# Attention scores by 32-row matmul tiles in four PSUM banks, and transposed probabilities in the turning banks

## What is computed

```python
def _L0_gnn_ref(x, adj_matrix, edge_attr_matrix, ...):
    nx = _ln(x, ln1_g, ln1_b)
    q = (nx @ wq + bq).reshape(b, s, H, HD).transpose(0, 2, 1, 3)      # H = 8, HD = 32; k and v alike
    bias = jnp.where(adj_matrix > 0, 0.1 * edge_attr_matrix * adjf, -jnp.inf)[:, None]
    scores = jnp.einsum('bhqd,bhkd->bhqk', q, k) / np.sqrt(HD) + bias
    attn = jax.nn.softmax(scores, axis=-1)
    out = jnp.einsum('bhqk,bhkd->bhqd', attn, v).transpose(0, 2, 1, 3).reshape(b, s, d)
    x1 = x + (out @ wo + bo)
    return x1 + jax.nn.gelu(_ln(x1, ln2_g, ln2_b) @ w1 + b1, approximate=False) @ w2 + b2

def _L1_gnn_ref(x, adj, ...):                  # attention again, with its own weights and mask adj == 0
    y = attention(x) @ Wo + bo + x
    return (y - mu) * jax.lax.rsqrt(var + EPS) * gamma + beta
```

## Time and profile before

| | |
|---|---|
| Median of 3 executions | 2414.14 us (2414.06 to 2414.62) |
| Profiled execution, its own time | 2410.11 us |
| Span of its core | 2408.0 us |
| TensorE matmul busy | 2332.9 us (97%) |
| TensorE weight loads busy | 1995.6 us (83%) |
| VectorE busy | 1940.4 us (81%) |
| ScalarE busy | 1694.6 us (70%) |
| GpSimd busy | 1106.0 us (46%) |

### The profile page before, as it was taken

How to read it: one execution, slowest core, us unless ns; L and a number is a source line. 1 busy time by engine, 2 the same in 40 slices (tenths; PEclk the granted TensorE clock), 3 DMA queues, 4 the chain that set the end, 5 groups by cost and what they waited for, 6 DMA issues and landing times.

```text
span 2408.0 us, 54142 instructions
## 1 busy us (share of the span) xinstructions
PE 2332.9 (97%) x17728; PEld 1995.6 (83%) x17728; DVE 1940.4 (81%) x8492; ACT 1694.6 (70%) x5646; POOL 1106.0 (46%) x1160
## 2 busy tenths in 40 slices
PE   4799999999999999999999999999999999999996
PEld 4688888888888888888888888888888888888875
DVE  5588888888888888888888888888888888888775
ACT  2567777777777777777777777777777777777774
POOL 2235444454454454454454454454454454454454
PEclk8899999999999999999999999999999999999999
DMA  4122212222212222212222212232222232222211
GB/s 129 36 68 71 71 47 59 79 78 66 71 47 61 77 79 65 71 49 66 70 80 65 71 50 66 69 80 65 71 54 62 69 80 65 73 57 59 58 49 42
DMA packets 172627, 159.35 MB, mean 66 GB/s; under 512 B 16832, under 2 KB 168000, under 8 KB 172352
## 3 DMA queue, kind: packets, MB, share of 16 engines
q1 hardware_dynamic: 172352, 155.91, 24.3%
HBM read 55.20 MB, written 16.78 MB: 30 GB/s over the span
## 4 chain that ended last, share of the span: by engine, by line
PE 88%; DVE 6%; ACT 2%; issue 1%; POOL 0%; POOLq 0%; DVEq 0%; ACTq 0%
PE p_bank L1029 56%; PE p_scores L1029 14%; PE p_probs L1122 8%; PE p_bank L1136 6%; PE p_bank L1047 4%; DVE x_two L708 3%; ACT scores L592 1%; DVE queries_a L817 1%; DVE scores L793 1%; DVE heads_t L863 1%; ACT heads_t L633 1%; DVE negmax L793 0%; DVE normed L813 0%; DVE x_two L742 0%; PE p_bank L980 0%
## 5 line engine op out<-in xcount | busy, mean ns | idle before, releaser
L542 POOL TENSOR_TENSOR scores<-scores,inverse 128x512 f32<-128x512 f32 x512 | 540.9, 1059 | 732.7 <-DVE inverse L803 732.7
L592 ACT ACTIVATE scores<-scores,negmax 128x128 f32<-128x128 f32 x2048 | 792.6, 391 | 23.1 <-DVE negmax L793 19.3
L592 ACT ACTIVATION_READ_ACCUMULATOR scores<-scores,negmax 128x1 f32 x2048 | 388.4, 190 | 0.0
L1029 PEld LDWEIGHTS p_bank<-w_down,hidden 128*128 128x128 f32 x3072 | 374.7, 191 | 8.9 <-issue 6.0
L1029 PE MATMUL p_bank<-w_down,hidden 128*128 128x256 f32 x3072 | 381.8, 284 | 0.0
L1029 PE MATMUL p_bank<-normed,w_up 128*128 128x512 f32 x1536 | 366.7, 395 | 1.9 <-DVE normed L813 1.9
L1029 PEld LDWEIGHTS p_bank<-normed,w_up 128*128 128x128 f32 x1536 | 285.3, 189 | 61.0 <-issue 2.1
L633 ACT ACTIVATE heads_t<-p_bank 128x256 fp32r<-128x256 f32 x256 | 98.6, 385 | 323.2 <-PE p_bank L1136 323.2
L1122 PE MATMUL p_probs<-ident,scores 128*128 128x128 f32 x2048 | 272.6, 276 | 2.8 <-POOL scores L542 2.8
L1122 PEld LDWEIGHTS p_probs<-ident,scores 128*128 128x128 f32 x2048 | 228.0, 141 | 33.4 <-issue 20.0
L616 ACT ACTIVATE p_bank<-p_bank,ready_cols 128x512 f32<-128x512 f32 x256 | 169.5, 662 | 122.0 <-PE p_bank L1029 116.3
(11 more groups left out here) (112 smaller groups left out, 3968.1 us busy)
## 6 DMA issues: line engine op xcount, KB each, us to landing
key_blocks<-hidden SPq DMA_DIRECT2D x512, 128.0 KB, 2.4
x_in<-in_x SPq DMA_DIRECT2D x32, 512.0 KB, 4.4
res_a<-in_x SPq DMA_DIRECT2D x32, 512.0 KB, 4.0
res_c<-x_two SPq DMA_DIRECT2D x32, 512.0 KB, 3.4
out<-res_c SPq DMA_DIRECT2D x128, 128.0 KB, 1.8
adj_a<-in_adj SPq DMA_DIRECT2D x32, 256.0 KB, 3.8
adj_c<-in_adj SPq DMA_DIRECT2D x32, 256.0 KB, 3.2
res_c<-in_L_gnn_w SPq DMA_DIRECT2D x1, 512.0 KB, 5.9
```

Source lines behind the costliest of these rows:

```text
L542: nc.gpsimd.tensor_tensor(rows_c, rows_c, inverse[:, k % 2, heads].unsqueeze(2).broadcast_to([P, HC, P]), ALU.mult).then_inc(probs_made, 1)
L592: last = nc.scalar.activation(scores[:, k % 2, h], scores[:, k % 2, h], ACT.Exp, scale=-1.0, bias=negmax[:, k % 2, h:h + 1], accum_out=tot ...
L1029: last = nc.tensor.matmul(dst, stationary(i), moving(j), start=(n == 0), stop=(n == total_n - 1))
```

## The change

The scores of each head are now a product of their own that reads 32 partitions of the queries and of the keys: 2 halves (c) x 3 passes x 4 heads (j), 24 matmuls with 128 columns. The head's place j sets the rows of the array and the bank: `p_scores` has four banks, one for each j, so that four neighbouring matmuls use four row groups and four banks. `key_blocks`, its DMAs and the waits for them go, and `keys` get tensors of their own for A and C. VectorE's mask waits once for all eight heads and then goes by groups g of four heads (j = 0, 1 and j = 2, 3), where it went by c.

With four banks for scores, `p_probs` goes. The two halves of a unit's transposes, (T, r, 0) and (T, r, 1), now each take one of the four turning banks. The orders change: TensorE makes T after `early` and `mid`, with W between the two halves. VectorE masks its second half before it evacuates the last step's Q1 or K1, and copies the second T half (`turned`) before it evacuates this step's Q0 or K0. ScalarE evacuates `early` and `mid`, then copies the first T half, then makes the second half of the exponentials (in the step with DOWN 1 it makes them first).

```diff
@@ Shape.__init__: numbering of the turning banks
-            self.number(self.first.get(k, []) + only("V", lag) + self.early.get(k, [])
-                        + self.mid.get(k, []) + only("W", lag) + self.fill.get(k, []))
+            self.number(self.first.get(k, []) + only("V", lag) + self.early.get(k, []) + self.mid.get(k, [])
+                        + [op + (0,) for op in only("T", lag)] + only("W", lag) + [op + (1,) for op in only("T", lag)]
+                        + self.fill.get(k, []))
...
-        p_scores = ctx.enter_context(nc.psum_tensor("p_scores", [P, KC, HC * P], F32))
-        p_probs = ctx.enter_context(nc.psum_tensor("p_probs", [P, KC, HC * P], F32))
+        p_scores = ctx.enter_context(nc.psum_tensor("p_scores", [P, HC, TOK], F32))
...
+        def score_columns(c, j):
+            return p_scores[:, j, c * P:(c + 1) * P]
+        def slot_of(c, j):
+            return HC * (j // 2) + 2 * c + j % 2
...
@@ VectorE body
-                    for op in s.fill.get(k - 1, []):
-                        if op[0] in ("Q", "K"):
-                            evacuate(t, op)
                     if k in s.units and k == s.behind:
                         mask_scores(t, k, 0)
                     if k in s.units:
                         mask_scores(t, k, 1)
+                    for op in s.fill.get(k - 1, []):
+                        if op[0] in ("Q", "K"):
+                            evacuate(t, op)
...
-                    for op in s.early.get(k, []):
+                    for op in s.early.get(k, []) + s.mid.get(k, []):
                         if op[0] == "DOWN":
                             prepare(t, k)
-                        evacuate(t, op)
+                        if op[0] in ("DOWN", "UP"):
+                            evacuate(t, op)
                     for _, r in only("T", lag):
                         turned(t, r)
+                    for op in s.early.get(k, []) + s.mid.get(k, []):
+                        if op[0] not in ("DOWN", "UP"):
+                            evacuate(t, op)
                     if k in s.units and k != s.behind:
                         invert(t, k, 1)
-                    for op in s.mid.get(k, []):
-                        evacuate(t, op)
...
@@ TensorE make_scores
-                    moving = lambda j: key_blocks[:, c, j, :, b * P:(b + 1) * P]
-                    stationary = lambda i: queries[stage][:, i, c, b * P:(b + 1) * P]
-                    three_passes(p_scores[:, c, :].rearrange("p (h n) -> p h n", h=HC), [(stationary, moving)]
-                                 ).then_inc(scores_made, 1)
+                    for n, (i, i2) in enumerate(passes):
+                        for j in range(HC):
+                            rows_j = slice(HD * j, HD * (j + 1))
+                            last = nc.tensor.matmul(score_columns(c, j), queries[stage][rows_j, i, c, tokens],
+                                                    keys[stage][rows_j, i2, c, tokens], start=(n == 0),
+                                                    stop=(n == len(passes) - 1))
+                last.then_inc(scores_made, 1)
+            def turn(t, r, g):
+                pe.wait_ge(probs_made, u * KC + g + 1)
+                bank, dst = take(t, ("T", r, g))
+                for n in range(HC):
+                    last = nc.tensor.transpose(dst[:, n * P:(n + 1) * P], scores[:, par, HC * g + n, :], ident[:, :])
+                last.then_inc(filled[bank], 1)
...
@@ TensorE body
-                    for op in s.early.get(k, []):
+                    for op in s.early.get(k, []) + s.mid.get(k, []):
                         work(t, op)
-                    for op, r in only("T", lag):
-                        lagging(t, op, r)
-                    for op in s.mid.get(k, []):
-                        work(t, op)
+                    for _, r in only("T", lag):
+                        turn(t, r, 0)
                     for op, r in only("W", lag):
                         lagging(t, op, r)
+                    for _, r in only("T", lag):
+                        turn(t, r, 1)
```

More of the change, by code:

```diff
@@ L187, in bank, with turned_bank @@
         return n % BANKS, self.grown(n // BANKS + 1, len(s.use) // BANKS)
+    def turned_bank(self, r, g):
+        key = ("T", r, g)
+        if key in self.s.use:
+            return self.bank(key)
+        return self.bank(("T", r + len(self.s.before.order), g), earlier=True)
     def high(self, key):
```

124 lines of the change are left out of this document (47 added, 77 removed).

## The result

The changed kernel takes 2713.56 us (median of 4 runs, 2706.93 to 2717.33), where the kernel before took 2414.10 us beside it. The ratio is 1.124 (95% interval 1.122 to 1.126): 12.4% slower. My forecast of 2664 us was 50 us too low, inside its range.

A forecast was written before the change was run, and what follows sets the result against it. TensorE was taken as the bound, 71.83 of 71.98 us a turn. Some 12.7 us of new waits less 4.9 of shorter scores made +7.8 us a turn, 250 us over 32 turns: 2664 us, range 2500 to 2880.

The forecast's parts named there:

- A block of scores, 0.86 us: The 24 score matmuls on TensorE: 0.86 us at O's pace of 0.036 us each, against 1.47 before.
- Steps 1 and 6, +1.80 each: W waits for K1's or Q1's evacuation, Q1 for Q0's behind the late T copy: 8.32 us against 6.52.
- Steps 0 and 5, +1.71 and +2.51: K0 waits for XT's low part, then W and K1 for banks: +1.71 us in step 0, +2.51 in step 5.
- Step 3, +0.69: UP 0 starts at 1.18 us; UP 2 waits for UP 1's bank: 1.30 less 0.61 is +0.69 us.
- Step 4, -0.61: Only shorter scores; DOWN 1 covers mask and exponentials, and W, T and XT find banks drained: -0.61 us.
- Steps 2 and 7, -0.05: W is held back until 3.14 us, but ScalarE empties V0 in time: 6.63 against 6.68 us, -0.05 each.
- The DMAs of `key_blocks` without effect: Dropping these DMAs saves nothing: they lay beside a busy TensorE, which had 0.15 us without work a turn.
- Busy 85 to 90%: Sign to look for: TensorE's busy share falls to some 85 to 90%, at a granted clock near 1.00.
- "I put nothing down for it": No cost for a clock drop in TensorE's new gaps, though worst steps idle some 2.4 of 8.3 us.
- the covered waits: Rival: bank waits are covered and busy time decides; 2258 us, or about 2320 if VectorE bounds; 14 in 100 together.
- That tiles don't overlap: Rival: row tiles run one after another, scores take 3.1 us, 3240 us in all; 6 in 100.
- the waits would be half of what I walked: Rival: VectorE gets ahead of the walk, or scores reach their lower bound: 2400 to 2500 us; 8 in 100.

The follow-up runs named there:

- the wide scores: Kernel before, with its six 512-column score matmuls and `key_blocks`, but the changed kernel's banks and orders: 2771.22 us, ratio 1.148.
- the second experiment: Changed kernel with the last step's Q1 or K1 evacuated by VectorE ahead of the second half of the mask: 2613.26 us, ratio 1.083.
- the two-bank version: Kernel before, its banks and orders kept, with row tiles in two score banks, heads one behind the other, without `key_blocks`: 2577.86 us, ratio 1.069.
- full rows: Changed kernel with each of the 24 score matmuls reading all 128 rows instead of 32 (another result): 3106.38 us, ratio 1.287.
- the scores twice: Changed kernel with every block of scores made twice, 48 matmuls into the same banks: 2807.22 us, ratio 1.163.

## Why the prediction was right, and where it was off

The predicted 2664 us is 50 us (1.9%) below the measured 2713.56, and the range held it. By its steps:

- **A block of scores, 0.86 us:** 0.82 measured. The estimate from O was right, and so was its reason, that tiles overlap: a 128-column matmul costs 0.11 us on its rows, and four go at once. My other price, 0.13 us overlapped by four, gave 0.79 and was as near. *The gain of 0.61 us a step* was a little too large, since the entry into row tiles was not counted (0.17 us behind XT).
- **Steps 1 and 6, +1.80 each:** step 1 took 8.44 us against 6.52, +1.92. The chain ahead of Q1 was 2.04 us for 2.07 walked. From the early T to W it was 1.15 us for 0.40 + 0.66. (A row's bracket is smaller than my wait, because it counts from the modelled end of the half T, 0.60 us, where I counted 0.40.) Step 6 took 9.69 us, +3.17; see the last point.
- **Steps 0 and 5, +1.71 and +2.51:** +1.82 and +2.40. K0 waits 0.49 and 1.07 us for `normed`, K1 1.44 in both, the mechanism as walked.
- **Step 3, +0.69:** +0.86. UP 0 and UP 2 wait 0.49 and 0.52 us.
- **Step 4, -0.61:** -0.68. **Steps 2 and 7, -0.05:** 0.00 in step 2, +0.46 in step 7. 0.29 of this is its start in the low clock, and 0.17 a slip of mine: I took the 6.68 us of step 2 for both, and step 7 had taken 6.51.
- **The DMAs of `key_blocks` without effect:** the packets moved 159 MB before and 93 MB after; the wide scores show 1.0 us of waits for them. The step holds.
- **Busy 85 to 90%:** 86%.
- **"I put nothing down for it", the clock:** this is the step that failed. I argued from the program's end, where the clock held at 1.00 with 2.65 of 5 us busy, that worst steps with 2.4 of 8.3 us idle would keep it. The prediction named a drop of the clock in the new gaps as a sign that it was wrong, and this sign came: the clock falls in every turn, behind steps 5 and 6 together. Its price is 46 us, by the groups of the second experiment and by the steps alike. In the windows, steps 6 and 7 are 1.9 us over my sum, 1.5 of them the clock, and the six others 0.3 together; times 32 that is 60 and 9 us, near the 57 by which the profiled execution was over (2717 for 2660). Without the clock the median would have been within a few us of the forecast, and that part was no luck: no two large errors cancel in the steps above.

The rivals: the covered waits fell at once, since the idle time stands in the trace at the places named. The warning of the Trainium skill ("TensorEngine Tiling (Array Packing)", PSUM Bottleneck) of copies out of PSUM as a bottleneck is borne out in a sense that I did not price: VectorE is not busier in sum (1945 us for 1940), but 22% of the chain lies on it. That tiles don't overlap is what the two-bank version half shows, at 2.04 us. That the waits would be half of what I walked was wrong.

Two causes are separated by the experiments. The loss comes from banks and orders (357 us with the wide scores), and the tiles give 58 us of a possible 123 (0.48 us in 256 blocks). In the changed kernel the place of one copy in VectorE's list makes 210 us, some 46 of them by the clock. What stays open: whether XT's low part could be made earlier without delaying the mask, and what exactly makes the clock fall. I can say what stood ahead of it, not what decides. It is not the wait ahead of Q1: with the same 88 us of it in all, the clock fell 30 times in the changed kernel, 29 with full rows, 14 with the scores twice, 8 with wide scores and never with K1 ahead of the mask. Nor is it TensorE's idle time in sum: 311 us with full rows and 342 with wide scores. So it isn't shown either that W's wait of 0.55 us as such made it fall; shown is that it fell in no turn when this wait was taken out.

## What to carry to other kernels

When PSUM banks are dealt out in turn, a product waits for whoever had its bank last, so ask for each use on which engine's list its evacuation stands and what is ahead of it there: moving one copy behind one evacuation was worth 210 us here, more than the whole new matmul form. Small tiles on separate rows went at once here with a bank for each, and lost with two banks and an order between them; count what gives up its banks for them. When a walk through the schedule leaves new gaps on TensorE, allow for the clock too, as a range: kernels with the same wait of 1.44 us ahead of Q1 lost from 0 to 46 us by it. And when two edits are weighed alone, look whether both give back the same clock; then their gains don't add.

## What the runs showed of the hardware

- Matmuls of 128 float32r columns on 32 rows start 0.11 us apart on the same rows, as full-row ones do (0.113 us), and four on different rows start within 30 ns. This held when three in a row of the list used the same rows. With six in a row per head and two banks, the second head started 0.28 us after the first. TensorE thus does start a matmul on free rows while earlier ones of its list wait for theirs, but not arbitrarily far ahead; how far, these runs don't tell.
- The step from full-row work to row tiles takes 0.17 us behind XT (0.96 against 0.79). Going on from them showed no such cost: O, which works in tiles of 32 columns, starts 0.20 us after the last score matmul with row tiles and with full rows alike.
- The granted clock fell once a turn (30 times) behind waits of 1.07, 1.44, 0.55 and 1.44 us, and in no turn when the 0.55 alone was gone. A fall made one product take 2.90 for 1.65 us and the scores behind it 1.19 for 0.89, 1.54 us in all. The same wait of 1.44 us ahead of Q1 went with 30, 29, 14, 8 and 0 falls in five kernels.
